# Window attention and spiking layer on one core: q and k projected a row further ahead, k's blocks placed by DMA, small tiles for maxima and picks

## The chip, the cores and the metric

The kernel runs on one core of a Trainium2 chip. The metric is the device time of one execution in microseconds, the median of several runs.

## The reference

`x` has 8 samples of 32 x 32 tokens with 256 channels.

```
x = x + attention(groupnorm(x))     # 8x8 windows, 16 heads of 16, bias table, mask -100
x = x + lif(groupnorm(x) @ W.T + b) # over the samples as time steps: charge, spike at >= 1, reset
attention: q, k, v = h @ qkv_w.T + qkv_b;  p = softmax(q*s @ k.T + bias + mask);  out = p @ v
```

A window has 64 tokens; four windows lie side by side in a window row, and the 8 samples have 32 such rows.

## The kernel before

Channels lie on the partitions (two halves `h` of 128), tokens in the free dimension. The attention goes through 32 window rows and, in each, two pairs of windows (`p` 0 and 1): 64 pairs, numbered `n`. The code of a sample is eight pairs long (`k` 0 to 7). Sample 0 and the last two are written out and the others are a loop. Every engine has its own `pair` function, a list in a fixed order, tied to the others by semaphores.

For a row, ACT normalises it (`normalise`, L478) and rounds it (`xn_high`, L490), POOL takes the rest (`low_part`, L403), and PE projects q, k (`project_q`, `project_k`, L918 to L923: 26 products of 128x256 4-byte elements) and v (`project_v`, L931 to L933: 12 products). q and k are then split into a high and a low f16 part: the high part by ACT (`q_high` L496, `k_high` L509), the low one by DVE (`q_low` L742, `k_low` L755). k is written twice, masked by the parity of the head (`parity_mask`), so that in each group of 32 channels one copy holds the even head and the other the odd one, with zeros between.

The score products (`scores`, L988 and L990, 32 per pair) need the three parts high x high, high x low, low x high under each other on 96 partitions. That is what `q_stack` and `k_stack` are (two slots of each). SP makes them through DRAM (`move_q_and_k`): it spills q and k (L321, L324, L315) and reads them back in stacks (L305). It also spreads q into `q_hi` (L311), whose zeros separate the heads for the maxima.

The softmax is made safe by a maximum for each query and head, taken one pair ahead: `max_scores` (L965 bias, L971 high parts) on PE, `maxima` (L772) on DVE, `turn_maxima` (L1005) on PE between the two halves of the next pair's scores, a copy into `max_rows` by ACT (L585), and at the end of the scores eight picks (L998), products that add the negated maximum of the right head to each score. ACT takes the exponential twice (L594 f32, L595 f16), POOL the rest (L441), PE multiplies with the values of the pair before (`weigh_values`, L1021), DVE divides (L786), PE turns the result (L1031), ACT keeps it (L558) and POOL adds it to x (L430).

In a pair PE does: the projection (q and k of the next row in even pairs, v of the next row in odd ones), scores with `turn_maxima`, picks, `weigh_values` of the pair before, `max_scores` of the next pair, `turn_attention`. After the attention the spiking layer runs through the 32 rows.

The two waits of `max_scores` and the one of `scores` are, in the code:

```
if k % 2 == 0:
    pe.wait_ge(k_hi_done, row + 1)
    pe.wait_ge(q_spread[slot], slot_total(row, k // 2, 64))
...
if p == 0:
    pe.wait_ge(stacked[slot], slot_total(row, k // 2, 96))
```

Of the kernel before, what the change touches and what calls it, by code (L numbers as in the profile page):

```python
# [3 lines left out]


def swin_attention_then_lif_kernel(nc, image, x, qkv_w, qkv_b, bias_table, lif_w, lif_b, out):
# [40 lines left out]
    with ctx:  # L47
# [3 lines left out]
        def sem(name):  # L51
# [14 lines left out]
        parity_mask = sb("parity_mask", [128, 2], f32)  # L66
        pick_max = sb("pick_max", [128, 2 * QUADS, 128], f16)
        bias_k = sb("bias_k", [128, 4, 2 * QUADS, 128], f16)
        bias_q = sb("bias_q", [128, 4, QUADS, 128], f16)
# [16 lines left out]
        bits = sb("bits", [128, 4], i32)  # L86
        flags = sb("flags", [128, 3], f32)
# [4 lines left out]
        q_hi = [sb(f"q_hi{i}", [128, HALVES, WCOLS, QUADS, WS], f16) for i in range(2)]  # L92
        q_stack = [sb(f"q_stack{i}", [96, QUADS, HALVES * WCOLS, WS], f16) for i in range(2)]
        k_stack = [sb(f"k_stack{i}", [96, QUADS, HALVES * WCOLS, 128], f16) for i in range(2)]
        q_spill = [[nc.dram_tensor(f"q_spill{i}{part}", [128, HALVES * ROWTOK], f16).ap() for part in ("hi", "lo")] for i in range(2)]
        k_spill = [[nc.dram_tensor(f"k_spill{i}{part}", [128, 2 * HALVES * ROWTOK], f16).ap() for part in ("hi", "lo")]
                   for i in range(2)]
        k_hi = [sb(f"k_hi{i}", [128, HALVES, WCOLS, 2, WS], f16) for i in range(2)]
        k_lo = [sb(f"k_lo{i}", [128, HALVES, WCOLS, 2, WS], f16) for i in range(2)]

        v_hi = [sb(f"v_hi{i}", [128, 2, HALVES * QUADS, 2, 2, D + 1], f16) for i in range(2)]
        v_lo = [sb(f"v_lo{i}", [128, 2, HALVES * QUADS, 2, 2, D + 1], f16) for i in range(2)]
# [52 lines left out]
        q_spread = [sem(f"q_spread{i}") for i in range(2)]  # L155
        q_hi_spilled = [sem(f"q_hi_spilled{i}") for i in range(2)]
        q_lo_spilled = [sem(f"q_lo_spilled{i}") for i in range(2)]
        k_hi_spilled = [sem(f"k_hi_spilled{i}") for i in range(2)]
        k_lo_spilled = [sem(f"k_lo_spilled{i}") for i in range(2)]
# [100 lines left out]
        BODY = 2 * WROWS  # L260

        W_SCALES = ((0, C, QK_SCALE), (C, 3 * C, 1.0))
# [22 lines left out]
        def _(sp):  # L285
# [58 lines left out]
            def pair(n, row, k, s):  # L344
# [4 lines left out]
                if k % 2 == 0 and not is_last_row(row):  # L349
                    move_q_and_k((k // 2 + 1) % 2, row + 1, k // 2 + 1)  # L350
# [112 lines left out]
        def _(act):  # L463
# [103 lines left out]
            def pair(n, row, k, s):  # L567
# [31 lines left out]
                if is_first(n, 2):  # L599
                    bias_high(2 + k)  # L600
# [528 lines left out]
```

## Time and profile before

| | us |
|---|---|
| median of 3 runs | 542.16 |
| lowest, highest | 538.04, 542.87 |
| the profiled execution's own time | 540.15 |
| its span, first to last instruction | 538.4 |
| PE, DVE, ACT, POOL busy in the span | 453.2, 426.7, 395.2, 274.1 |

The attention runs from the first pair at about 43 us to about 470 us, the spiking layer to the end. The span is 1.75 us shorter than the execution's time. Busy time is not work at full rate: products on PE are pipelined, each takes some 0.2 us from start to end and the next one starts 0.03 to 0.12 us after it.

### The profile page before, as it was taken

What the parts mean: (1) busy time and instruction counts of PE and PEld (TensorE: products, weight loads), DVE (VectorE), ACT (ScalarE), POOL (GpSimd) and SP (SyncE); (2) the same over time, 40 slices, a digit from 0 to 9 for tenths busy, and PEclk for the clock granted to TensorE, in tenths of its full rate; (3) what the DMA queues carried; (4) which work ended last, traced back from release to release, by engine and by line L of the source; (5) the groups of instructions that cost most, each with busy time, mean ns of one, the idle gap of its engine ahead of it and who ended that gap; (6) DMA issues with size and microseconds to landing.
All of it is one profiled execution on the core that took longest, in us unless ns stands there. A gap on an engine that the chain in (4) does not pass through costs nothing.

```text
span 538.4 us, 17562 instructions
## 1 busy us (share of the span) xinstructions
PE 453.2 (84%) x6504; PEld 415.6 (77%) x6504; DVE 426.7 (79%) x864; ACT 395.2 (73%) x885; POOL 274.1 (51%) x370
## 2 busy tenths in 40 slices
PE   0275689888989899989998999899899978789996
PEld 0164578887879788878888888899798867678885
DVE  6856568887887888878987898789877777588887
ACT  1375678887888788878887888788788856656551
POOL 6133565557555755666656656666665555540000
PEclk9988789999999999999999999999999989999999
DMA  6258066776777677767786788686666656023333
GB/s 191 83 142 199 12 177 167 185 191 168 186 180 176 172 179 197 188 170 182 202 203 156 198 196 195 159 196 162 160 157 168 163 144 157 2 84 133 136 136 138
DMA packets 92574, 86.07 MB, mean 160 GB/s; under 512 B 41842, under 2 KB 63604, under 8 KB 92532
## 3 DMA queue, kind: packets, MB, share of 16 engines
q1 hardware_dynamic: 91808, 85.49, 60.8%
q8 instruction: 27, 0.44, 0.4%
q10 hardware_dynamic: 724, 0.01, 0.1%
q14 instruction: 15, 0.12, 0.1%
HBM read 47.72 MB, written 33.55 MB: 151 GB/s over the span
## 4 chain that ended last, share of the span: by engine, by line
PE 36%; issue 17%; POOL 16%; ACT 10%; SPq 7%; DVE 7%; DMA 6%; ACTq 1%; POOLq 1%; DVEq 0%
POOL p_lo L441 7%; DMA k_stack<-k_spill1lo 4%; PE pv_ps L1021 4%; POOL xn_lo L403 3%; POOL xc L430 3%; PE score_ps L998 3%; PE proj_ps L921 3%; SPq L305 3%; SPq L311 3%; PE proj_ps L923 3%; PE proj_ps L908 3%; PE pv_ps L908 3%; PE score_ps L908 3%; PE proj_ps L922 3%; PE max_ps L908 2%
## 5 line engine op out<-in xcount | busy, mean ns | idle before, releaser
L441 POOL TENSOR_TENSOR p_lo<-probs,p_hi 128x512 f16<-128x512 f32 x128 | 146.6, 1167 | 151.9 <-ACT p_hi L595 151.9
L594 ACT ACTIVATE probs<-score_ps 128x512 f32<-128x512 f32 x128 | 76.9, 601 | 18.4 <-PE score_ps L998 17.6
L921 PE MATMUL proj_ps<-xn_hi,w_hi 128*128 128x256 f32 x256 | 77.0, 301 | 14.9 <-POOL xn_lo L403 14.9
L988 PE MATMUL score_ps<-both_parts,bias_k 128*128 128x64 f16 x1024 | 78.0, 193 | 11.7 <-DMA k_stack<-k_spill1lo 5.5
L988 PEld LDWEIGHTS score_ps<-both_parts,bias_k 128*128 128x128 f16 x1024 | 69.7, 98 | 16.8 <-issue 9.4
L772 DVE TENSOR_REDUCE neg_max<-max_ps 128x16 f16<-128x1024 f32 x64 | 78.4, 1225 | 3.7 <-PE max_ps L971 1.7
L990 PE MATMUL score_ps<-q_stack,k_stack 96*128 96x64 f16 x1024 | 77.7, 193 | 0.0
L595 ACT ACTIVATE p_hi<-score_ps 128x512 f16<-128x512 f32 x128 | 77.3, 604 | 0.0
L922 PE MATMUL proj_ps<-xn_lo,w_hi 128*128 128x256 f32 x256 | 74.1, 290 | 0.0
L923 PE MATMUL proj_ps<-xn_hi,w_lo 128*128 128x256 f32 x256 | 73.6, 287 | 0.0
L990 PEld LDWEIGHTS score_ps<-q_stack,k_stack 96*128 96x128 f16 x1024 | 69.1, 98 | 0.0
L755 DVE SCALAR_TENSOR_TENSOR k_lo<-proj_ps,parity_mask,k_hi 128x512 f16<-128x512 f32 x64 | 45.1, 746 | 26.8 <-ACT k_hi L509 26.8
L766 DVE TENSOR_TENSOR v_lo<-proj_ps,v_hi 64x256 f16<-64x256 f32 x128 | 54.1, 422 | 12.8 <-ACT v_hi L517 10.7
L921 PEld LDWEIGHTS proj_ps<-xn_hi,w_hi 128*128 128x128 f32 x256 | 50.3, 196 | 16.7 <-POOL xn_lo L403 9.8
L998 PE MATMUL score_ps<-max_rows,pick_max 128*128 128x128 f16 x512 | 40.5, 223 | 19.5 <-ACT max_rows L585 17.4
L517 ACT ACTIVATE v_hi<-proj_ps 64x256 f16<-64x256 f32 x128 | 50.5, 394 | 8.5 <-PE proj_ps L933 7.0
L786 DVE TENSOR_TENSOR attn<-pv_ps,recip 64x256 f32<-64x256 f32 x128 | 54.1, 422 | 3.1
L1021 PE MATMUL pv_ps<-v_hi,p_hi 128*128 128x68 f16 x512 | 55.6, 196 | 0.5 <-POOL p_lo L441 0.5
L1021 PE MATMUL pv_ps<-v_hi,p_lo 128*128 128x68 f16 x512 | 55.8, 196 | 0.0
L1021 PE MATMUL pv_ps<-v_lo,p_hi 128*128 128x68 f16 x512 | 55.7, 195 | 0.0
L509 ACT ACTIVATE k_hi<-proj_ps,parity_mask 128x512 f16<-128x512 f32 x64 | 40.5, 684 | 20.4 <-PE proj_ps L923 20.4
L403 POOL TENSOR_TENSOR xn_lo<-xn,xn_hi 128x512 fp32r<-128x512 f32 x32 | 41.1, 1285 | 22.8 <-ACT xn_hi L490 22.7
(137 smaller groups left out, 1354.6 us busy)
## 6 DMA issues: line engine op xcount, KB each, us to landing
xc<-in_x_dram SPq DMA_DIRECT2D x32, 256.0 KB, 4.9
k_stack<-k_spill0hi SPq DMA_DIRECT2D x32, 256.0 KB, 4.3
k_stack<-k_spill1hi SPq DMA_DIRECT2D x32, 256.0 KB, 4.3
out_dram<-xc SPq DMA_DIRECT2D x32, 256.0 KB, 2.3
q_hi<-q_flat SPq DMA_DIRECT2D x128, 32.0 KB, 2.0
k_spill0hi<-k_hi SPq DMA_DIRECT2D x16, 256.0 KB, 2.2
k_spill0lo<-k_lo SPq DMA_DIRECT2D x16, 256.0 KB, 2.3
q_stack<-q_spill0hi SPq DMA_DIRECT2D x32, 128.0 KB, 2.7
```

What stands on the lines that cost most here:

```text
L403: pool.tensor_tensor(xn_lo[slot][:, :], xn[slot][:, :], xn_hi[slot][:, :].bitcast(f32), ALU.subtract)\
L441: pool.tensor_tensor(p_lo[p][:, quads, :, :].rearrange("p g w i -> p (g w i)"), probs[:, quads, :, :].rearrange("p g w i -> p (g w i)"), p ...
L594: act.activation(probs[:, quads, :, :].rearrange("p g w i -> p (g w i)"), score_ps[:, h, :], ACT.Exp)
L595: act.activation(p_hi[p][:, quads, :, :].rearrange("p g w i -> p (g w i)"), score_ps[:, h, :], ACT.Exp)\
L772: dve.tensor_reduce(neg_max[:, 0:16], max_ps[:, :, :].rearrange("p w (n j) -> p (w n) j", j=WS), AX.X, ALU.max, negate=True).then_inc(neg_ ...
L908: last = pe.matmul(dst, w_lif[:, c, h * 128:(h + 1) * 128], tokens[:, c * ROWTOK:(c + 1) * ROWTOK], start=False, stop=(c == HALVES - 1))
L921: pe.matmul(dst, w_hi[:, c, cols], high[:, tok], start=(c == 0 and bias is None), stop=False)
L922: pe.matmul(dst, w_hi[:, c, cols], low[:, tok], start=False, stop=False)
L923: last = pe.matmul(dst, w_lo[:, c, cols], high[:, tok], start=False, stop=(c == HALVES - 1))
L988: pe.matmul(dst, bias_k[:, variant(k, w), h * QUADS + g, :], both_parts[:, 0, :], start=(g == 0 and w == 0), stop=False)
L990: pe.matmul(dst, k_stack[slot][:, g, at, :], q_stack[slot][:, g, at, :], start=False, stop=False)
L1021: last = pe.matmul(cols[:, :, g, :], pp[p][:, h * QUADS + g, :, :].rearrange("p w i -> p (w i)"), vv[k // 2][:, p, h * QUADS + g, :, :, :] ...
```

## The change

It has three parts.

- **Order.** q and k of row r + 2 are projected in the odd pair of row r, and v of row r + 1 in the even pair (before: q and k of row r + 1 in the even pair, v in the odd one). Normalising moves with it: `normalise` of row r + 3 at the end of ACT's odd pair, `xn_high` and `low_part` of row r + 2 in the even pair. v gets four buffers. On PE `max_scores` of the next pair stands right behind the picks, ahead of `weigh_values`, and its wait (now for the whole stack) stands before the last score product; on DVE `maxima` stands ahead of `attention_out`.
- **q and k.** k's high and low part are written once, flat, by one instruction each. The channels of q and k are permuted when the weights are prepared (4 x 3 small copies on ACT and on DVE in place of two large ones, four more small loads of biases), so that a stack is contiguous in DRAM for q. For k two DMAs per part put the even and the odd head's block into stacks that POOL has zeroed. A fourth group of 32 partitions is filled for half of the quads. q is no longer spread.
- **Tiles.** Maxima and picks use 64 rows and 64 columns of PE's array per product: 8 products of 256 columns for the bias and 16 of 128 for the scores' high parts (before: 2 of 512 and 8 of 128), and 16 picks of 128 (before: 8).

```
+            def stack_k(slot, first, part, quads=slice(0, QUADS)):
+                for e in range(2):
+                    rows = slice(first + e * D, first + (e + 1) * D)
+                    sp.dma_start(k_stack[slot][rows, quads, :, e * WS:(e + 1) * WS],
+                                 k_spill[slot][part][e * D:(e + 1) * D, quads, :].rearrange("d g (n j) -> d (g n) j", j=WS))\
+                      .then_inc(stacked[slot], 16)
+            def move_q_and_k(slot, r):
+                sp.wait_ge(q_flat_done, r + 1)
+                spill(q_flat, 0, q_hi_spilled, q_spill[slot][0])
+                sp.wait_ge(k_hi_done, r + 1)
+                spill(k_flat, 0, k_hi_spilled, k_spill[slot][0])
+                sp.wait_ge(k_lo_done, r + 1)
+                spill(q_flat, 1, q_lo_spilled, q_spill[slot][1])
+                if not is_first(r, 2):
+                    sp.wait_ge(score_ps_done, 4 * (r - 2) + 4)
+                spill(k_flat, 1, k_lo_spilled, k_spill[slot][1])
+                sp.wait_ge(q_hi_spilled, (r + 1) * 16)
+                stack_q(slot, 32, 0)
+                stack_q(slot, 64, 0)
+                stack_q(slot, 96, 0, slice(2, QUADS))
+                sp.wait_ge(k_hi_spilled, (r + 1) * 16)
+                stack_k(slot, 0, 0)
+                stack_k(slot, 32, 0)
+                stack_k(slot, 96, 0, slice(2, QUADS))
+                sp.wait_ge(q_lo_spilled, (r + 1) * 16)
+                stack_q(slot, 0, 1)
+                sp.wait_ge(k_lo_spilled, (r + 1) * 16)
+                stack_k(slot, 64, 1)
...
-                for e in range(2):
-                    last = act.activation(k_hi[slot][:, :, :, e, :].rearrange("p h w j -> p (h w) j"),
-                                          proj_ps[:, 1, :].rearrange("p (n j) -> p n j", j=WS), ACT.Identity,
-                                          scale=parity_mask[:, e:e + 1])
-                last.then_inc(k_hi_done, 1)
+                act.activation(k_flat[:, 0, :], proj_ps[:, 1, :], ACT.Copy).then_inc(k_hi_done, 1)
...
+            def max_scores(k):
+                slot = k // 2 % 2
+                halves = [slice(r * WS, (r + 1) * WS) for r in range(2)]
                 for w in range(2):
+                    for mid, rows in enumerate(halves):
+                        for q, queries in enumerate(halves):
+                            pe.matmul(max_ps[queries, mid, w * 256:(w + 1) * 256], ident_h[rows, rows],
+                                      bias_q[rows, variant(k, w), q, :, :].rearrange("p h n -> p (h n)"),
+                                      start=(w == 0), stop=False)
+                for w in range(2):
                     for h in range(HALVES):
+                        col = (2 * w + h) * 128
+                        at = h * WCOLS + 2 * (k % 2) + w
+                        for mid, rows in enumerate(halves):
+                            for q, queries in enumerate(halves):
+                                last = pe.matmul(max_ps[queries, mid, col:col + 128], q_stack[slot][rows, 2 * mid + q, at, :],
+                                                 k_stack[slot][rows, 2 * mid + q, at, :],
+                                                 start=False, stop=(w == 1 and h == 1))
...
+                for w in range(2):
+                    for h in range(HALVES):
+                        for mid, rows in enumerate(halves):
+                            for e, keys in enumerate(halves):
+                                dst = score_ps[keys, mid, :].rearrange("p (h q w i) -> p h w q i", h=2, q=2, w=2)[:, h, w, :, :]
+                                last = pe.matmul(dst, pick_max[rows, 2 * w + h, keys],
+                                                 max_rows[p][rows, :].rearrange("p (q i) -> p q i", q=2),
+                                                 start=False, stop=(w == 1 and h == 1))
+                            if w == 1 and h == 1:
+                                last.then_inc(score_ps_done, 1)
...
+                def await_tile_operands():
+                    pe.wait_ge(max_rows_done, n + 1)
+                    if not is_last_pair(n):
+                        await_max_operands(*following)
+                scores(n, row, k, await_tile_operands)
...
+                if not is_last_pair(n):
+                    max_scores(following[2])
                 if not is_first(n, 1):
+                    weigh_values(n - 1, row if p else row - 1, (k - 1) % BODY, beside)
```

PE before, in the loop, at the end of a pair: the last value products of the pair before, the maxima of the next pair (bias L965, scores L971), the turned attention, and the next projection.

```order
L1021 MATMUL pv_ps<-v_lo,p_hi 128x2x34
L1021 MATMUL pv_ps<-v_hi,p_lo 128x2x34
L960 REGISTER_ALU
L965 MATMUL max_ps<-bias_q,ident_h 128x512
L971 MATMUL max_ps<-k_hi,q_hi 128x128 x4
L965 MATMUL max_ps<-bias_q,ident_h 128x512
L971 MATMUL max_ps<-k_hi,q_hi 128x128 x4
L1031 MATMUL proj_ps<-ident,attn 128x128 x2
```

PE now, at the end of a pair's scores: the last score products (L1012, L1016), the picks (L1026), the maxima of the next pair (L987, L996) and the first value product.

```order
L1012 MATMUL score_ps<-both_parts,bias_k 128x64
L976 REGISTER_ALU
L1016 MATMUL score_ps<-q_stack,k_stack 128x64
L1026 MATMUL score_ps<-max_rows,pick_max 64x2x64 x16
L987 MATMUL max_ps<-bias_q,ident_h 64x256 x8
L996 MATMUL max_ps<-k_stack,q_stack 64x128 x16
L1040 REGISTER_ALU
L1050 MATMUL pv_ps<-v_hi,p_hi 128x2x34
```

The maxima moved ahead of the 24 value products and stand directly behind the picks; both read other operands and have more and smaller products.

SP before, one row in the loop: spills, spreads and stacks of one row.

```order
L321 DMA q_spill1hi<-q_flat 128x512
L311 DMA q_hi<-q_flat 32x8x64 x2
L324 DMA q_spill1lo<-q_flat 128x512
L315 DMA k_spill1hi<-k_hi 128x1024
L311 DMA q_hi<-q_flat 32x8x64 x2
L315 DMA k_spill1lo<-k_lo 128x1024
L305 DMA q_stack<-q_spill1hi 32x4x512 x2
L305 DMA k_stack<-k_spill1hi 32x4x1024 x2
L305 DMA q_stack<-q_spill1lo 32x4x512
L305 DMA k_stack<-k_spill1lo 32x4x1024
```

SP now, one row in the loop (L308 spills, L311 stacks of q, L317 stacks of k).

```order
L308 DMA q_spill1hi<-q_flat 128x512
L308 DMA k_spill1hi<-k_flat 128x512
L308 DMA q_spill1lo<-q_flat 128x512
L330 ISA
L308 DMA k_spill1lo<-k_flat 128x512
L332 REGISTER_ALU
L311 DMA q_stack<-q_spill1hi 32x2048 x2
L311 DMA q_stack<-q_spill1hi 32x1024
L317 DMA k_stack<-k_spill1hi 16x32x64 x4
L317 DMA k_stack<-k_spill1hi 16x16x64 x2
L311 DMA q_stack<-q_spill1lo 32x2048
L317 DMA k_stack<-k_spill1lo 16x32x64 x2
```

The four spreads are gone; k's three stacks of 2 KB pieces have become eight transfers of 128-byte pieces, of which six have 16x32 = 512 and two 16x16 = 256. The low part of k waits for the scores of the pair in which the row is projected.

## Rows read from the trace of the kernel before

**Rows 1.** One steady sample by stretches: us, busy us of engines, granted clock, DMA share, GB/s
```profile
286.67:337.66 50.99, 47.43 (x773) 43.81 (x773) 42.97 (x89) 43.16 (x101) 31.25 (x42) 1.00 0.75 186
```

**Rows 2.** Waits of PE from 108 to 467 us: us in total, times, longest
```profile
PE proj_ps L921 <- POOL xn_lo L403: 7.0, 6, 1.2
PE score_ps L998 <- ACT max_rows L585: 6.8, 17, 0.4
PE max_ps L1005 <- DVE neg_max L772: 5.8, 8, 1.0
PE score_ps L988 <- DMA k_stack<-k_spill1lo: 5.5, 6, 2.1
PE score_ps L988 <- DMA k_stack<-k_spill0lo: 4.0, 5, 1.8
PE pv_ps L891 <- DVE moments L686: 3.1, 1, 3.1
```

**Rows 3.** Timeline of PE within one pair: start, us
```profile
252.06 0.19 PE L990 MATMUL score_ps<-q_stack,k_stack 96*128 96x64 f16 x1
252.66 0.62 PE L998 MATMUL score_ps<-max_rows,pick_max 128*128 128x128 f16 x8 [0.42 <-ACT max_rows L585]
253.12 0.19 PE L1021 MATMUL pv_ps<-v_hi,p_hi 128*128 128x68 f16 x1
...
253.87 0.38 PE L965 MATMUL max_ps<-bias_q,ident_h 128*128 128x512 f16 x1
...
254.75 0.39 PE L1031 MATMUL proj_ps<-ident,attn 128*128 128x128 f32 x2
```

**Rows 4.** Timeline of ACT before the same picks
```profile
251.20 1.27 ACT L509 ACTIVATE k_hi<-proj_ps,parity_mask 128x512 f16<-128x512 f32 x2 [0.53 <-PE proj_ps L923]
252.36 0.25 ACT L585 ACTIVATE max_rows<-max_ps 16x128 f16<-16x128 f16 x1
```

**Rows 5.** Groups by line and shape: busy us, mean ns, idle before
```profile
L755 DVE SCALAR_TENSOR_TENSOR k_lo<-proj_ps,parity_mask,k_hi 128x512 f16<-128x512 f32 x64 | 45.1, 746 | 26.8 <-ACT k_hi L509 26.8
...
L509 ACT ACTIVATE k_hi<-proj_ps,parity_mask 128x512 f16<-128x512 f32 x64 | 40.5, 684 | 20.4 <-PE proj_ps L923 20.4
```

**Rows 6.** Timeline of SP's DMA issues within one row
```profile
189.54 0.43 SPq L315 DMA_DIRECT2D k_spill1hi<-k_hi  x1
190.01 1.26 SPq L311 DMA_DIRECT2D q_hi<-q_flat  x2
191.31 0.60 SPq L315 DMA_DIRECT2D k_spill1lo<-k_lo  x1
...
194.35 0.43 SPq L305 DMA_DIRECT2D k_stack<-k_spill1lo  x1
```

**Rows 7.** DMA issues: KB each, median us from issue to landing
```profile
k_stack<-k_spill0hi SPq DMA_DIRECT2D x32, 256.0 KB, 4.3
...
q_hi<-q_flat SPq DMA_DIRECT2D x128, 32.0 KB, 2.0
k_spill0hi<-k_hi SPq DMA_DIRECT2D x16, 256.0 KB, 2.2
```

**Rows 8.** The start: chain, PE's first maxima, SP's first stack, PE's wait for max_rows
```profile
4.40 8.23 DMA probs<-in_qkv_b_dram
...
36.21 0.38 PE L965 MATMUL max_ps<-bias_q,ident_h 128*128 128x512 f16 x1 [3.68 <-ACT bias_q L525]
...
34.83 0.94 SPq L305 DMA_DIRECT2D q_stack<-q_spill0hi  x2
...
PE score_ps L998 <- ACT max_rows L585: 10.6, 3, 5.2
```

**Rows 9.** Timeline of PE in a projection with 4-byte weights
```profile
248.86 0.28 PE L923 MATMUL proj_ps<-xn_hi,w_lo 128*128 128x256 f32 x1
248.98 0.28 PE L921 MATMUL proj_ps<-xn_hi,w_hi 128*128 128x256 f32 x1
```

More of the change, by code:

```diff
@@ L3 @@
 from contextlib import ExitStack
+import itertools
 def swin_attention_then_lif_kernel(nc, image, x, qkv_w, qkv_b, bias_table, lif_w, lif_b, out):
@@ L433, in pair @@
                 p = k % 2
-                if p == 1 and not is_last_row(row, 2):
+                if p == 0 and not is_last_row(row, 2):
                     low_part(k // 2 % 2, row + 3)
@@ L533, in _ @@
             for first, end, scale in W_SCALES:
-                act.activation(w_hi[:, :, first:end], w_raw[:, :, first:end], ACT.Copy, scale=scale).then_inc(setup_act, 1)
+                for c, h in itertools.product(range(HALVES), range(HALVES)):
+                    last = act.activation(w_columns(w_hi, first, c, h, True), w_columns(w_raw, first, c, h, False), ACT.Copy, scale=scale)
+                last.then_inc(setup_act, 1)
             act.activation(w_lif[:, :, :], w_raw[:, :, 3 * C:OUTS], ACT.Copy, scale=1.0 / TAU)
@@ L598, in pair @@
                     keep_attention(n - 2, p)
+                if is_first(n, 1):
+                    v_high(1, 2, 0)
+                    v_high(1, 2, 1)
+                if p == 1 and not is_last_row(row, 3):
+                    sample = s + (k // 2 + 3) // WROWS
+                    normalise(row + 3, sample, nxt % 2, sample + 1, row + 3)
                 if is_first(n, 2):
@@ new lines, in scores @@
+                for mid in range(2):
+                    wait(pe, p_hi_done, n * 2 + (mid - 1))
+                    for h in range(HALVES):
+                        for q in range(2):
+                            for w in range(2):
+                                col = (2 * h + q) * 128 + w * WS
+                                dst = score_ps[:, mid, col:col + WS]
+                                at = h * WCOLS + 2 * p + w
+                                pe.matmul(dst, bias_k[:, variant(k, w), h * QUADS + 2 * mid + q, :], both_parts[:, 0, :],
+                                          start=(h == 0 and q == 0 and w == 0), stop=False)
+                                if (mid, h, q, w) == (1, 1, 1, 1):
+                                    before_tiles()
+                                pe.matmul(dst, k_stack[slot][0:96, 2 * mid + q, at, :], q_stack[slot][0:96, 2 * mid + q, at, :],
+                                          start=False, stop=False)
+                    if mid == 0:
+                        turn_maxima(n)
```

339 lines of the change are left out of this document (146 added, 193 removed).

## The prediction

> **What bounds the kernel now.** First the view of the span by stretches, for one sample of the steady part [rows 1]. The reader is to see three things in it: the sample takes 50.99 us, PE is busy for 47.43 of them at a granted clock of 1.00 (the upper level, 2.4 GHz), while DVE and ACT have 8 us to spare and POOL 20. So PE's stream of instructions sets the pace, and the time is what PE issues plus what it waits for. The waits follow [rows 2], from the first steady sample (108 us) to the last pair (467 us): 7.0 us for POOL's xn_lo, 6.8 for ACT's max_rows, 5.8 for DVE's neg_max, 5.5 and 4.0 for the last transfer into k_stack, 3.1 for the moments of the last norm. That is 32.2 us of 359, over 28 rows; the rest is issue. The timeline of one pair [rows 3] shows what is issued: from the picks on, 0.46 us for eight picks, 0.75 us for 24 value products, 0.88 us for the score products of the next pair's maxima. It also shows a stretch without work of 0.6 us (252.06 to 252.66) between the last score product and the first pick.
>
> **The change on PE.** Per pair it takes away 8 picks and 10 products for maxima, which are 0.46 + 0.88 = 1.34 us [rows 3], and puts 16 picks and 24 products on 64x64 tiles in their place, 40 in all. No product on a part of the array that another product could share in time is in this trace, so the price is bounded. From the columns: 2048 columns for maxima took 0.88 us, 0.43 ns each [rows 3]. The new ones stream 16 x 128 + 8 x 256 + 16 x 128 = 6144 columns. If the four tiles work at once this is 1536 columns, 0.66 us per pair, or -0.68 x 64 pairs = -43 us; if nothing overlaps it is 2.64 us, +1.30 x 64 = +83 us. The nearest row is the smallest product with its own weights: 24 value products from 253.12 to 253.87, 31 ns each although they stream only 68 columns [rows 3]. I take this as what a load of weights and a short product cost together: 40 x 31 = 1.25 us, -0.09 x 64 = -6 us.
>
> **The change in the waits.**
> - *xn_lo*: normalising and splitting a row now comes a half row before the q projection that reads it (its low part on POOL in the even pair, the projection in the odd one). The 7.0 us go. Next late is the norm of the next sample, which must be ready at the end of pair 3 instead of at pair 4.
> - *neg_max*: the maxima of pair n + 1 are now multiplied right after the picks of pair n and reduced before the attention output. They come about 0.75 us earlier on PE and 1.2 us earlier on DVE, more than the usual lateness: 5.8 us go.
> - *max_rows*: k's high part was two ACT instructions, 1.27 us on ACT's queue ahead of max_rows [rows 4, 5], and becomes one. Its group says 684 ns each, so some 0.6 us of the queue go, and max_rows starts when it is turned. A part stays in every pair, since the turned maxima must go through ACT and back; in [rows 3] the wait was 0.42, and I leave a third of it: -5 of the 6.8 us.
> - *k_stack*: the stacks are filled one row further ahead, so the 9.5 us go if SP keeps up. This is the dearest condition. SP issued 15 transfers a row, and now issues 17: 4 spills, 4 of q, 8 of k, one of x. Such an issue takes 0.43 us where it moves 128 pieces, and 0.63 us each where it moves 256 pieces of 128 bytes (the spread of q, two in 1.26 us) [rows 6]. Six of the new k transfers move 512 pieces of 128 bytes, two move 256. An issue of 512 lies between 0.43 us (the count does not matter) and 0.43 + 3 x 0.20 = 1.03 us (each further 128 pieces cost what the first ones did). I take 0.63, the nearest row. From the start of the projection of q and k the k_low spill may start after about 5.3 us (3.2 us of projection, 1.0 us of scores, 0.3 to 0.6 us of waiting, 0.46 us of picks, for it now waits for the scores of this pair to free the slot). Then SP needs 0.45 for it, 4 x 0.47 for q, 8 x 0.63 for k: 12.7 us. A transfer of 128-byte pieces landed after 2.0 us, the k stacks after 4.3 [rows 7], so all is there at 14.7 to 17.0 us. PE asks after one row and 4.3 us more; with a row of 11.9 us that is 16.2. It just holds. What is queued behind that wait on PE is everything: the last score product, picks, maxima.
>
> A rule of the Trainium skill speaks against these pieces: its page "DMA: Bandwidth & Descriptors", Specifications, wants at least 512 B per piece for full rate. The spread's 32 KB landed in 2.0 us against 2.2 for 256 KB of k in 2 KB pieces [rows 7], so small pieces do lose rate here. That the load on the 16 engines stays bearable follows from the share of 0.75 [rows 1] and the fewer bytes.
>
> Together -7.0 - 5.8 - 5 - 9.5 = -27 us.
>
> **What it adds.** DVE loses one of its two k_low passes (746 ns, [rows 5]), which only shortens the chain to SP. When PE stops waiting, ACT is next: in the sample it was busy 43.16 us, and loses 4 x 0.6; a sample of 47.4 - 0.4 + small waits leaves it 6 us free, but the even pair, with v's four copies, is the tight one. I give back 3 us for it. At the start the first maxima were multiplied at 36.21 us, right after q's spread [rows 8]; now they wait for all 12 stack transfers. SP began its stacks at 34.83 us [rows 8]; 4 x 0.47 + 8 x 0.63 = 6.9 us and a landing put the first maxima at about 44 us, 8 us later, and the projection of the second row stands behind them. Part of this is taken up, since PE waited 10.6 us for max_rows there while the bias tables were made, which goes on beside it. The start itself waited till 12.63 us for the small loads of the biases (begun at 4.40, [rows 8]), behind four more issues now. I take +5 us for the start, from 0 to +10. The 12 small copies of the permuted weights lie beside the first statistics.
>
> **Sum**, against the profiled execution's 540.15 us (2.0 us below the median of the runs shown): 540.15 - 6 - 27 + 3 + 5 = 515 us. Against the median it would be 517; I say 516.
>
> **Rivals.**
> 1. *The tiles work four abreast* (chance 0.22). For it: the fixed cost of a product is not tied to its columns in [rows 3], so the columns could vanish. Against it: 31 ns looks like a floor. Then 43 us go instead of 6: 515 - 37 = 478, but the even pair then runs into ACT, of which I keep 10 us: 488.
> 2. *SP comes too late* (0.20), the case on the slow side. One mechanism: the eight k issues. At 1.03 us for 512 pieces the chain above is 5.3 + 0.45 + 1.9 + 6 x 1.03 + 2 x 0.63 = 15.1 us, and 17.1 to 19.4 with landing, against 16.2 that PE leaves. With 3 us of landing each row is 1.9 us too long, 28 x 1.9 = +53 over 515, or 568; halfway to the bound it is about 548. The rows are hidden up to an issue of 0.72 us, and from 0.87 us on (0.9 us per row, 25 us in all) nothing of the gain is left. For it: an issue of 256 pieces did take longer than one of 128 [rows 6]. Against it: the issue after a spread takes 0.60 too, so it may be a matter of form, not of count.
> 3. *Weights of a tile load at the slow rate* (0.10). Products with 4-byte weights of 128 columns follow at 0.12 us [rows 9] though their 256 columns need only 0.11 at 0.43 ns. If tile weights load like these and one after another, half the columns take 60 ns: 40 x 60 = 2.4 us per pair, +1.06 x 64 = +68 where I took -6: 589.
> 4. *The waits only change their names* (0.10): the arrays' change of shape and ACT take back what goes, 0.2 us per pair and the rest in waits for max_rows: 540.
>
> Rival 3 is also what the Trainium skill would have: "TensorEngine Tiling (Array Packing)", Restrictions and Gotchas, says that column tiling excludes the fast load of weights, and "TensorE: Matmul & The Clock Gate", LDWEIGHTS, prices a load by its columns, which for 64 columns would be an estimated 53 ns. The trace agrees in that 2-byte weights of 128 columns keep a 31 ns rhythm and 4-byte ones do not. The first page also says that tiles load and multiply in parallel, which is rival 1.
>
> **How the numbers follow.** The forecast (505 to 530) has 0.38, rivals 1 to 4 0.22, 0.20, 0.10 and 0.10. The predicted time is the forecast's, 516. About 1% is what a measurement of this kernel can tell from no change. Faster by more: the forecast, rival 1 and 0.02 of the milder end of rival 2: 0.62. Within 1%: most of rival 4 and a part of rival 2, 0.13. Slower: the rest, 0.25. The range takes in rival 1 and the milder half of rival 2, and leaves rival 3 out: 485 to 562.
>
> **What would show it.** In the profile of the changed kernel: PE's waits for xn_lo and neg_max gone from the list; 16 picks and 24 maxima products from first to last in about 1.25 us per pair (0.7 is rival 1, 2.4 is rival 3); a steady sample of about 47.5 us; no wait for a k_stack transfer; SP's issues of k near 0.63 us. The first maxima near 44 us. The forecast is wrong if SP has no idle time within a row, or if PE's wait before the last score product of odd pairs names a k_stack transfer in the steady samples.

## The result, and the profile after

| | before | after |
|---|---|---|
| median of the runs, us | 540.88 (538.04 to 542.87) | 547.35 (546.37 to 548.88) |
| profiled execution, us | 540.15 | 546.64 (span 544.9) |

The ratio is 1.0117 (95% interval 1.0069 to 1.0165): the changed kernel is slightly slower. 516 us were predicted, with 0.62 on faster. Times here and below are medians of all executions of a kernel, while a ratio and its interval leave out those that are over 1.5% above the fastest of their kernel; so the 540.3 us of the first experiment stand beside a ratio of 0.9948.

The waits of PE from 113 to 472 us, the answer to [rows 2]:

```profile
PE score_ps L1016 <- ACT max_rows L598: 28.9, 23, 1.5
PE proj_ps L949 <- issue: 11.4, 4, 3.0
PE score_ps L1016 <- DMA k_stack<-k_spill1lo: 5.3, 6, 3.0
PE score_ps L1016 <- DMA k_stack<-k_spill0lo: 4.9, 6, 1.5
PE pv_ps L909 <- DVE moments L703: 0.8, 1, 0.8
PE max_ps L1034 <- DVE neg_max L785: 0.2, 1, 0.2
```

xn_lo and neg_max have gone from the list, as forecast. The wait for max_rows has grown from 6.8 to 28.9 us, the k_stack waits are 10.2 where they were 9.5, and there is a new kind: four waits of nearly 3 us before the v projection with no releaser at all ("issue": the profile shows nothing that PE waited for). The sum is 51 us, where it was 32.

The timeline of PE in one pair, the answer to [rows 3]:

```profile
379.48 0.20 PE L1016 MATMUL score_ps<-q_stack,k_stack 96*128 96x64 f16 x1 [1.31 <-ACT max_rows L598]
379.62 0.42 PE L1026 MATMUL score_ps<-max_rows,pick_max 64*64 64x128 f16 x16
379.86 0.39 PE L987 MATMUL max_ps<-bias_q,ident_h 64*64 64x256 f16 x8
380.08 0.39 PE L996 MATMUL max_ps<-k_stack,q_stack 64*64 64x128 f16 x16
380.41 0.20 PE L1050 MATMUL pv_ps<-v_hi,p_hi 128*128 128x68 f16 x1
```

Read the starts, not the durations: 16 picks, 8 bias products and 16 score products take from 379.62 to 380.41, 0.79 us, where the old ones took 1.34. So the tiles are cheap. By the single starts four products begin together; the next four follow 0.056 us later where a product has 128 columns, and 0.11 us later where it has 256, so columns set the pace and not the loads of weights. But ahead of them PE stands 1.31 us for max_rows. ACT over the same stretch, the answer to [rows 4]:

```profile
376.66 1.12 ACT L493 ACTIVATE xn<-xc,shift,rstd 128x256 f32 x2
377.82 0.63 ACT L506 ACTIVATE xn_hi<-xn 128x512 fp32r<-128x512 f32 x1
378.35 0.77 ACT L529 ACTIVATE v_hi<-proj_ps 64x256 f16<-64x256 f32 x2
379.15 0.28 ACT L598 ACTIVATE max_rows<-max_ps 128x128 f16<-128x128 f16 x1
```

The maxima were turned at 377.5; the normalising, xn_hi and the first half of v_hi stand ahead of their copy in ACT's queue. This is the even pair; in the odd one ACT is idle for nearly 2 us. k's copies are cheaper, as forecast: one of 0.60 us on ACT and one pass of DVE, the answer to [rows 5]:

```profile
L773 DVE TENSOR_TENSOR k_flat<-proj_ps,k_flat 128x512 f16<-128x512 f32 x32 | 22.1, 690 | 7.0 <-ACT k_flat L524 7.0
```

SP's issues of one row (the last column counts the issues that the duration spans), and the landing of the k stacks, the answers to [rows 6, 7]:

```profile
239.90 0.35 SPq L308 DMA_DIRECT2D q_spill1hi<-q_flat  x1
240.31 0.42 SPq L308 DMA_DIRECT2D k_spill1hi<-k_flat  x1
240.78 0.46 SPq L308 DMA_DIRECT2D q_spill1lo<-q_flat  x1
242.37 0.32 SPq L308 DMA_DIRECT2D k_spill1lo<-k_flat  x1
242.81 2.70 SPq L311 DMA_DIRECT2D q_stack<-q_spill1hi  x3
245.56 3.72 SPq L317 DMA_DIRECT2D k_stack<-k_spill1hi  x6
249.31 0.45 SPq L311 DMA_DIRECT2D q_stack<-q_spill1lo  x1
249.81 2.43 SPq L317 DMA_DIRECT2D k_stack<-k_spill1lo  x2
...
k_stack<-k_spill1lo SPq DMA_DIRECT2D x32, 64.0 KB, 3.3
```

In this row 12.3 us pass from the first spill to the end of the last issue (10.3 to 13.0 in the others); there is a gap of 1.1 us before the k_low spill, where SP waits for the slot. The spans of three and of two issues, 2.70 and 2.43 us, hide something. Single issues into k_stack from 110 to 465 us, shortest, median and longest in ns, before and after:

```profile
L305 SPq DMA_DIRECT2D k_stack<-k_spill1hi x28: 430/432/438, 113.4 to 452.6; - x28
L317 SPq DMA_DIRECT2D k_stack<-k_spill1hi x84: 447/626/1805, 113.1 to 454.5; - x84
L317 SPq DMA_DIRECT2D k_stack<-k_spill1lo x28: 544/627/1897, 117.4 to 457.4; - x28
```

Most issues of 512 pieces take 0.63 us, as the prediction had it. But 47 of SP's 449 issues in this stretch take 1.0 to 2.1 us, where it was 10 of 391 before; in the row above it is one of the q issues and one of the k_low ones, 1.84 us each. Why these are long is open. How much room is left on SP is told by its wait for the next row's q, before and after:

```profile
SPq L321 <- ACT q_flat L496: 115.7, 26, 8.9
SPq L308 <- ACT q_flat L512: 14.6, 12, 3.0
```

Before, SP was done ahead of the next q in 26 of 28 rows and waited 4.4 us each time in the mean. Now rows take 12.4 to 13.5 us, and it is done ahead of the next q in 12 of 28.

Samples by stretches, the answer to [rows 1]: a looped one, and the last but one, which is written out in the program:

```profile
275.00:327.70 52.70, 45.65 (x952) 43.00 (x950) 39.24 (x84) 40.90 (x97) 31.37 (x41) 0.95 0.54 131
377.50:426.90 49.40, 43.69 (x954) 41.21 (x951) 37.62 (x80) 40.72 (x97) 31.14 (x42) 1.00 0.51 119
```

PE's busy time at the full clock has fallen from 47.43 to 43.69 us a sample. The written-out sample is 1.6 us shorter than one of before, the four looped ones at whose end the loop turns (52.7 to 54.1) are 2 to 3 longer. The fifth looped one, which has no turn behind it, takes 49.8. What happens at the first turn, at 162 us, in steps of 2 us (clock: third number from the end), and the wait itself:

```profile
162.00:164.00 2.00, 0.22 (x2) 0.00 (x0) 1.92 (x6) 2.00 (x6) 2.00 (x2) 1.00 0.56 148
164.00:166.00 2.00, 0.97 (x8) 0.98 (x9) 0.98 (x4) 0.89 (x2) 1.72 (x3) 1.00 0.38 82
166.00:168.00 2.00, 2.00 (x31) 1.90 (x31) 0.35 (x1) 0.97 (x3) 0.37 (x1) 0.60 0.41 61
168.00:170.00 2.00, 2.00 (x54) 1.73 (x52) 1.49 (x5) 1.65 (x5) 0.00 (x0) 0.55 0.57 107
170.00:172.00 2.00, 2.00 (x35) 2.00 (x36) 1.83 (x5) 1.83 (x5) 1.61 (x2) 1.00 0.53 98
```

```profile
165.03 0.38 PE L949 MATMUL proj_ps<-w_hi,xn_hi 128*128 128x256 f32 x1 [2.81 <-issue]
```

PE stands still for 2.81 us, works on, and then the granted clock is at its lower level (1.2 GHz) for most of four microseconds. The same follows each of the four turns: the missing shares of the clock over the 2 us steps add up to 8.5 us of lost time, in the loop of before to nothing. A hint at the wait is the queue that brings instructions to the engines. From 165 to 300 us it carries no packet in the trace of before, and in that of after:

```profile
q8 instruction: 23, 0.38, 1.3%
```

At the start the forecast held: the first maxima were multiplied at 45.18 us (44 forecast), after the wait below, the answer to [rows 8], and the second sample began 4.7 us later than before (5 forecast).

```profile
PE max_ps L987 <- DMA k_stack<-k_spill0lo: 10.4, 1, 10.4
```

### The profile page after: what moved, and what is told of

Read it like the earlier page. It is cut to its first block, busy times and chain, and to the rows that moved or that the text cites. A ratio compares the mean times of both kernels' runs of the same rounds, so it can differ in the third digit from the quotient of the medians.

```text
span 544.9 us, 20474 instructions
## 1 busy us (share of the span) xinstructions
PE 434.2 (80%) x7912; PEld 403.4 (74%) x7912; DVE 398.2 (73%) x838; ACT 377.4 (69%) x863; POOL 280.3 (51%) x382
## 4 chain that ended last, share of the span: by engine, by line
PE 38%; SPq 21%; ACT 11%; DMA 10%; issue 9%; DVE 8%; ACTq 1%; POOL 0%; DVEq 0%; POOLq 0%
SPq L317 12%; SPq L311 7%; DMA k_stack<-k_spill0lo 4%; PE pv_ps L1050 4%; PE proj_ps L939 3%; DMA k_stack<-k_spill1lo 3%; PE proj_ps L940 3%; PE proj_ps L941 3%; PE score_ps L1026 3%; PE score_ps L1016 3%; PE proj_ps L926 3%; PE pv_ps L926 3%; PE score_ps L926 3%; ACT xn L493 2%; ACT v_hi L529 2%
## 5 line engine op out<-in xcount | busy, mean ns | idle before, releaser
L1016 PE MATMUL score_ps<-q_stack,k_stack 96*128 96x64 f16 x1024 | 88.1, 197 | 50.5 <-ACT max_rows L598 39.2
L1016 PEld LDWEIGHTS score_ps<-q_stack,k_stack 96*128 96x128 f16 x1024 | 74.2, 100 | 56.8 <-ACT max_rows L598 47.7
L779 DVE TENSOR_TENSOR v_lo<-proj_ps,v_hi 64x256 f16<-64x256 f32 x128 | 54.2, 423 | 59.3 <-ACT v_hi L529 58.4
L1012 PE MATMUL score_ps<-both_parts,bias_k 128*128 128x64 f16 x1024 | 80.8, 197 | 0.0
L1012 PEld LDWEIGHTS score_ps<-both_parts,bias_k 128*128 128x128 f16 x1024 | 72.8, 100 | 2.8
L1050 PEld LDWEIGHTS pv_ps<-v_hi,p_hi 128*128 128x128 f16 x512 | 49.4, 101 | 5.5 <-POOL p_lo L454 1.0
L940 PEld LDWEIGHTS proj_ps<-xn_lo,w_hi 128*128 128x128 f32 x256 | 50.8, 198 | 0.0
L941 PEld LDWEIGHTS proj_ps<-xn_hi,w_lo 128*128 128x128 f32 x256 | 50.5, 197 | 0.0
```

The costliest lines, as they stand in the source:

```text
L940: pe.matmul(dst, w_hi[:, c, cols], low[:, tok], start=False, stop=False)
L941: last = pe.matmul(dst, w_lo[:, c, cols], high[:, tok], start=False, stop=(c == HALVES - 1))
L1012: pe.matmul(dst, bias_k[:, variant(k, w), h * QUADS + 2 * mid + q, :], both_parts[:, 0, :], start=(h == 0 and q == 0 and w == 0), stop=False)
L1016: pe.matmul(dst, k_stack[slot][0:96, 2 * mid + q, at, :], q_stack[slot][0:96, 2 * mid + q, at, :], start=False, stop=False)
L1050: last = pe.matmul(cols[:, :, g, :], pp[p][:, g // 2 * 4 + h * 2 + g % 2, :, :].rearrange("p w i -> p (w i)"), vv[k // 2][:, p, h * QUADS ...
```

## The experiments

Three theories stood at first: A, the loop's body no longer stays with PE and is fetched at each turn; D, ACT's queue in the even pair makes PE late; E, the chain of SP's issues does. B, C and F are named in the expectations. Kernel 7 is the kernel of experiment 7, and so on. Each kernel is compared with runs of the kernel before on the same chip.

**1. The loop written out** (after, one edit).

```diff
-            with eng.Fori(1, SAMPLES - 2) as s:
-                for k in range(BODY):
-                    body(s * BODY + k, s * WROWS + k // 2, k, s)
-            for s in (SAMPLES - 2, SAMPLES - 1):
+            for s in range(1, SAMPLES):
```

> The changed kernel with its loop over samples 1 to 5 written out in the program, nothing else. Theory A (the loop's body, 952 products a sample instead of 773, no longer stays with TensorE and is fetched again at each turn: four waits before the v projection with no releaser, 11.4 us in all): these waits go, 547.4 becomes about 536; if the slower pace of the looped samples (53.5 us each against 49.6 of the written-out ones) is the fetch too, 527. Rival B (the waits at the turn only take the place of others, and the pace is set by ScalarE and the stacks): 545 to 549, with other waits at the same places. Rival C (straight code is fetched all the time as well, at its own price): 547 or more, with waits without a releaser spread over the samples.

540.3 us (533.0 to 542.6, 10 runs), 0.9948 [0.9907, 0.9989] of before. The waits without a releaser are gone; those for max_rows and the k stacks have grown from 38 to 52 us (both from 112 to 470 us):

```profile
PE score_ps L1013 <- ACT max_rows L595: 33.9, 27, 1.4
PE score_ps L1013 <- DMA k_stack<-k_spill0lo: 9.1, 8, 2.0
PE score_ps L1013 <- DMA k_stack<-k_spill1lo: 8.7, 8, 1.9
```

So A is right that these waits come with the loop, and B about more than half of their worth in this kernel: of 11.4 + 8.5 us, 7 to 9 came out as time.

**2. The kernel before with about as many products as after** (control for A: 969 a sample, after 952): each maxima product cut in two, each pick in four or two.

```diff
+                            for e in range(2):
+                                last = pe.matmul(max_ps[:, w, at + e * WS:at + (e + 1) * WS],
...
+                            parts = 4 - 2 * w
+                            for c in range(parts):
```

> The kernel before with the products of its maxima cut in two and those of its picks in four or two, 24 more products a pair and the same columns, so that its loop body is as long as that of the changed kernel (which has 22 more a pair). Theory A: the instruction queue, quiet in the loop of before, carries packets all through the loop and TensorE waits without a releaser at the four turns; 540.9 becomes 550 or more (11 for the fetch, up to 5 for the cut products). Rival: the length of the body means nothing, no such waits, and 541 to 546 by the cuts alone.

582.2 us, 1.0747 [1.0678, 1.0815]. The instruction queue is at work in the loop, and the first line of PE's waits is

```profile
PE proj_ps L921 <- issue: 19.8, 4, 5.1
```

Before had no such line. The four looped samples with a turn take 59.3 to 61.0 us, the two behind the last turn 52.6 and 53.0 (before 50.7 and 51.6), so the turns cost some 30 us: 19.8 of waits, and the rest goes with the lower clock, whose missing shares add up to 12. The cut products cost 1.6 a sample. Here only the number of products was changed, and the waits came: that they hang on the size of the loop's body is shown, at a price above the expectation. That the wait is a fetch is read from the queue's packets.

**3. Full-array picks in the changed kernel** (looped; 8 products of 128x128 in place of 16 tiles).

```diff
-                            for e, keys in enumerate(halves):
-                                last = pe.matmul(dst, pick_max[rows, 2 * w + h, keys],
+                            last = pe.matmul(dst, pick_max[:, 4 * mid + 2 * w + h, :],
```

> The changed kernel, in its loop, with eight picks over the full 128x128 array a pair instead of sixteen in 64x64 tiles; the maxima's 24 products stay tiles. Price of a tile: eight full picks stood at 0.46 us a pair in the kernel before, sixteen tile picks take 0.247 us, so TensorE's busy time rises by 0.21 x 64 = 14 us (by nothing if tiles only overlap in pairs, as the prediction had it: 16 x 31 ns = 0.50). The loop's body has 64 products a sample fewer (888 against 952 and 773 before): if its length decides the fetch in proportion, the waits without a releaser at the turns fall from 11.4 to about 7 us; if there is a size from which all of it is fetched again, they stay at 11 or vanish. Time: 547 to 560.

554.2 us, 1.0214 [1.0122, 1.0306]. The eight picks last from 391.65 to 392.20, 0.55 us against 0.247 for 16 tiles (379.62 to 379.86 above): the tiles overlap four abreast.

```profile
391.65 0.61 PE L1024 MATMUL score_ps<-max_rows,pick_max 128*128 128x128 f16 x8
392.20 0.41 PE L986 MATMUL max_ps<-bias_q,ident_h 64*64 64x256 f16 x8
```

The waits without a releaser did not shrink with the body (15.9 us in all at 888 products a sample, 11.4 at 952, none at 779). That reads as a size from which the body is fetched, between 779 and 888 products, each with its load of weights; these are two different kernels, and nothing between was run.

**4. The kernel before, written out** (control; the edit of 1).

> The kernel before, written out, as a control: its loop showed no packet of the instruction queue and no wait without a releaser. Theory A: 540.9 stays within 3 us, since there is nothing to gain and straight code runs without a stall. If straight code costs by itself, it is slower by over 3 us.

548.4 us, 1.0107 [1.0042, 1.0172]: a miss, straight code is not free here. No wait lacks a releaser; the k_stack waits rose from 9.5 to 17.0 us. Why the stacks land later is open.

**5. ACT's normalising earlier** (after, looped): its two operations move ahead of k's copy in the odd pair.

```diff
                     q_high(row + 3)
+                    if not is_last_row(row, 3):
+                        normalise(row + 3, sample, nxt % 2, sample + 1, row + 3)
                     k_high(row + 3)
```

> The changed kernel with ScalarE's two normalising operations (1.12 us) moved from the end of the odd pair into its idle time ahead of k's copy. Theory D (in the even pair ScalarE's queue, normalise + xn_hi + v_hi ahead of max_rows, makes TensorE's last score product late by 28.9 us in all): that wait falls by about 1 us a row, 20 to 28 us in all, and the time falls by 12 to 25 us, to 522 to 535. Rival E (the row's period is set by the stacks, which SyncE issues too late: 9 of its issues of 512 pieces at 0.62 to 0.83 us): the max_rows wait falls, the k_spill waits before the maxima's products grow by as much, and the time stays within 3 us of 547.

573.5 us, 1.0614 [1.0559, 1.0669], against both theories. The edit made a wait of its own: in the second row of a sample the normalising needs the next sample's scales, which POOL has not done:

```profile
191.02 1.09 ACT L493 ACTIVATE xn<-xc,shift,rstd 128x256 f32 x2 [4.15 <-POOL shift L237]
```

Behind it stand k's copy and max_rows, so PE stands still from 188.61 to 192.88, and its clock is at half from 190 to 197, so it falls before PE goes on. This comes in each sample: six ACT waits of 23.9 us, and the granted clock is 0.88 to 0.92 in four samples. PE's busy time rose from 434 to 447 us for the same products.

**6. The same, written out** (the edits of 1 and 5).

> Both edits, loop written out and normalise early. If theories A and D hold and are independent their gains add: 547 - 11 - 12 to 25 = 511 to 524. If one hides behind the other (both stand on the same chain of a row), the time is that of the better one of the two, 525 to 536. If E holds for the row's period, about that of the written-out kernel alone.

562.7 us, 1.0363 [1.0303, 1.0423]. Writing out takes some 11 us off kernel 5; the wait for the scales is there too. It tells nothing on D and E.

**7. Normalising early in three rows of four** (written out).

```diff
-                    if not is_last_row(row, 3):
+                    if k != 3 and not is_last_row(row, 3):
```

> The changed kernel written out, with the two normalising operations ahead of k's copy in three rows of four; in the second row of each sample they stay behind, since there they would wait for the next sample's scales (the ScalarE wait of 4.2 us that the first try of this had in each sample). Theory D (ScalarE's queue in the even pair): the max_rows wait falls from 33.9 to some 10 us and the time from 540.3 to 515 to 525. Rival E (SyncE's issues and the landing of the stacks set the row): the k_stack waits grow from 17.8 us by as much as the max_rows wait falls; 535 to 542. Theory F (the clock, granted at half for some 4 us behind each stall of TensorE of nearly 3 us): no window of 2 us below 0.98 in the steady part, since no wait of over 2 us is left.

538.2 us (534.6 to 544.7), 0.9912 [0.9870, 0.9954]. The max_rows wait fell by 22 us and the k_stack waits rose by 14:

```profile
PE score_ps L1016 <- DMA k_stack<-k_spill0lo: 18.3, 13, 2.5
PE score_ps L1016 <- DMA k_stack<-k_spill1lo: 13.4, 9, 3.5
PE score_ps L1016 <- ACT max_rows L598: 11.8, 18, 1.4
```

So D's wait is real, but its end is worth 2 us, which the intervals of kernels 1 and 7 can't tell from nothing, and the k_stack waits take its place, as E has it. SP is the fuller for it: it is done ahead of the next q in 4 rows.

```profile
SPq L305 <- ACT q_flat L509: 2.5, 4, 1.2
```

F failed: the clock fell three times in the steady samples, at 214, 330 and 368 us, behind k_stack waits of 2.25, 1.55 and 1.77 us.

**8. SP's chain relieved**: kernel 7, where the stacks' rows 96 to 127 are not loaded any more from the third row on, one q and two k transfers a row less. The products still read them, so for half of the heads the maxima leave out this row's high product.

```diff
-                stack_k(slot, 96, 0, slice(2, QUADS))
+                if r < 2:
+                    stack_k(slot, 96, 0, slice(2, QUADS))
...
```

(the q transfer likewise)

> The same, and from the third row on the stacks' rows 96 to 127 are not loaded any more (one q and two k transfers a row less, of 9 SyncE issues of 512 pieces... two less); what is left out is the high product of half the heads in the maxima. It prices SyncE's chain: three issues less are 0.46 + 2 x 0.79 = 2.0 us a row on SyncE. Rival E: the k_stack waits go, and the time is 10 to 25 us under that of the kernel that loads them. Theory D alone: the same within 3 us.

504.5 us (501.8 to 508.8), 0.9333 [0.9251, 0.9414], 34 us under kernel 7. The k_stack waits are down from 31.7 to 4.6 us, and all steady samples look alike:

```profile
295.10:341.10 46.00, 43.63 (x953) 41.16 (x950) 39.40 (x86) 40.30 (x97) 31.26 (x42) 1.00 0.61 141
```

E is shown for a kernel whose ACT order is mended: PE is busy for as long as in kernel 7, but is not kept waiting. SP is done ahead of the next q in 18 rows (20.4 us of waiting). Two things stay open. The three transfers have gone from the DMA engines too, and not only their issues from SP; kernel 11 bears on that. And the same relief with ACT's order as in the changed kernel was not run, so how much of the 34 us needs both is not known.

**9. The kernel before, relieved alike**: two of its six stack transfers a row left out from the third row on, and with them two parts of the scores' operands. That is 0.9 us of SP a row, where kernel 8 has some 2.0.

```diff
-                stack(1, k_stack[slot], k_spill[slot][0])
+                if is_first(row, 2):
+                    stack(1, k_stack[slot], k_spill[slot][0])
```

(likewise `stack(2, q_stack[slot], q_spill[slot][0])`)

> The kernel before with two of its six stack transfers a row left out from the third row on (third q part and second k part of the scores' sum: left out of the computation), 0.43 us of SyncE each. The same relief of the chain that gave the changed kernel 34 us. If TensorE bounds the kernel before (47.2 us of 51 a sample), only the k_stack waits of 8.4 us can go: 530 to 541. If the stacks' chain set the pace there too, 505 to 525, and the change's gain on TensorE was not hidden by a bound that it brought itself.

536.9 us (535.3 to 538.5), 0.9918 [0.9890, 0.9947]. Its k_stack waits shrank to 0.2 us (its max_rows waits grew from 6.8 to 11.2), and nothing more was to be had:

```profile
208.90:259.90 51.00, 47.33 (x778) 43.88 (x775) 42.98 (x89) 43.11 (x101) 31.21 (x41) 1.00 0.60 154
```

This is the clearest comparison of the study. With the chain out of the way, the kernel before takes 51.0 us a sample and the changed one (with ACT's order mended, written out) 46.0, 536.9 against 504.5 us. The gain is there, and the chain that came with the change hides it: before, PE was the bound, and SP had time to spare.

**10. Kernel 8 in its loop** (the edit of 1 taken back).

> The kernel without the stacks' rows 96 to 127 (what is left out is the high product of half the heads in the maxima), in its loop instead of written out, the only difference from the kernel of 504.5 us. There TensorE is the bound (46 us a sample, 43.6 busy), so the fetch at the turns has its full price: four waits of 2.8 to 3 us and half the clock for some 4 us behind each, 11.4 + 8.5 = 20 us: 520 to 528. Rival: the waits are made good by slack (as most of them were in the changed kernel, where writing out gave 7 us): 508 to 512.

523.9 us, 0.9668 [0.9615, 0.9721]: 19.4 us over kernel 8 for the loop alone, more than twice as much as in experiment 1, since here little else is waited for. PE's waits without a releaser are 14.5 us, and a looped sample shows the clock:

```profile
161.70:212.30 50.60, 44.80 (x951) 42.16 (x949) 39.25 (x84) 40.18 (x97) 31.22 (x41) 0.97 0.56 127
```

**11 to 14. A version that keeps the whole computation.** Kernel 7 with the four q transfers of a row issued by POOL (11), the same issued behind xn_lo (12), that with max_rows ahead of the first v_hi on ACT (13), and that with POOL's issues back behind p_lo and the addition of the attention behind xn_lo (14).

```diff
...
+                    pool.wait_ge(q_hi_spilled, (row + 3) * 16)
+                    stack_q(pool, q_stacked[slot], slot, 32, 0)
+                    stack_q(pool, q_stacked[slot], slot, 64, 0)
+                    stack_q(pool, q_stacked[slot], slot, 96, 0, slice(2, QUADS))
+                    pool.wait_ge(q_lo_spilled, (row + 3) * 16)
+                    stack_q(pool, q_stacked[slot], slot, 0, 1)
```

For 13, on ACT:

```diff
-                if v_now:
-                    v_high(nxt, row + 2, 0)
                 act.wait_ge(max_turned, n + 1)
                 act.activation(max_rows[p][:, :], max_ps[:, 0, :].bitcast(f16)[:, 0:128], ACT.Copy)\
                     .then_inc(max_rows_done, 1)
                 if v_now:
+                    v_high(nxt, row + 2, 0)
                     v_high(nxt, row + 2, 1)
```

For 14, on POOL:

```diff
                     low_part(k // 2 % 2, row + 3)
+                if p == 0 and not is_first(n, 3):
+                    add_attention(n - 3, row - 2, 1)
```

> The same as the early normalising in three rows of four, with the four q transfers of a row issued by GpSimd instead of SyncE (1.8 us a row off SyncE's chain, nothing left out). Rival E: the k_stack waits fall by 1 to 2 us a row against the kernel that issues all from SyncE, 5 to 20 us in all. Against it: GpSimd issues slower than 1 us a transfer, p_lo comes late, and pv_ps waits for it: the time is 5 to 20 us worse.

> The written-out kernel with the early normalising and the four q transfers from GpSimd, now issued behind xn_lo in the next pair instead of ahead of it (2.0 us of GpSimd's issues stood before xn_lo, and TensorE waited for xn_lo 25.0 us in all, once a row). If that wait only came from the order on GpSimd, it falls to under 5 us and the time from 530.9 to 507 to 517, as the k_stack waits stay away. If the later q transfers become the last to land, a wait for q_stack or k_stack takes its place and the time stays at 525 to 532. Nothing is left out.

> The kernel with the later q transfers, and on ScalarE max_rows ahead of the first v_hi in the even pair (0.77 us). If ScalarE's queue is what is left of the max_rows wait (12 us), it falls to under 6 us and the time by 3 to 8 us; if v_lo and through it the next q projection become late by it (v_lo on VectorE, then the wait of TensorE on v_lo), the same within 2 us.

> The kernel of 529.3 us (written out, early normalising, max_rows first) with GpSimd's q transfers issued at once behind p_lo of the odd pair (there no stack was waited for), and the addition of the attention put behind xn_lo (0.74 us earlier xn_lo). If the row is now set only by the order on GpSimd, q_stack and k_stack waits fall from 19.6 to under 5 us, the xn_lo wait is 5 to 18 us (1.3 less 0.74 us a row), and the time is 510 to 525. If the stacks' chain sets it whatever GpSimd does, 526 to 532 with the waits under other names.

| kernel | us | ratio to before | what PE waits for most, us |
|---|---|---|---|
| 11 | 530.9 | 0.9811 [0.9744, 0.9878] | xn_lo 25.0, max_rows 12.6, k_stack 1.9 |
| 12 | 532.0 | 0.9796 [0.9741, 0.9852] | q_stack 21.5, max_rows 12.0, k_stack 7.1 |
| 13 | 529.3 | 0.9781 [0.9719, 0.9843] | k_stack 14.8, v_lo 10.8, q_stack 4.8 |
| 14 | 526.0 | 0.9725 [0.9677, 0.9773] | xn_lo 20.0, no releaser 7.2, k_stack 4.8 |

Kernel 11 takes nothing out, only moves 1.8 us a row off SP, and the k_stack waits fall from 31.7 to 1.9 us. A row on SP takes some 9 us there, where it was 11 to 13 in kernel 7, and SP waits 69.8 us in all for q: the stacks were late by SP's time, and not by what the transfers put on the DMA engines. (In part they have more time, too: PE stands 1.0 us a row for xn_lo, ahead of the projection that they follow.) POOL's 2.0 us stand ahead of xn_lo now; issued later, as in 12, they make the q transfers the last to land. Kernel 13 missed the 3 to 8 us (the intervals overlap with 12), though the max_rows wait fell to 3.9 us. Kernel 14 is the best that computes everything: it beats the kernel before by 2.7% and the changed one by about 21 us. Its steady samples take 49.4 us in the mean, where kernel 8, which loads less, takes 46.0.

## Why the prediction was wrong, by its own steps

- *Tiles, -6 us.* Failed, in its size: the value products' 31 ns a product were taken for a floor. 40 products took 0.79 us a pair, not 1.25, and 16 tile picks 0.247 against 0.55 for 8 full ones. Rival 1, four abreast at 0.66, was the nearer. By the starts this is 0.55 x 64 = 35 us, by PE's busy time per sample (47.43 to 43.69) 30.
- *xn_lo and neg_max, -7.0 and -5.8.* Right.
- *max_rows, -5.* Failed: +22. The step looked at k's copy, which is in the odd pair. In the even pair the normalising, xn_hi and half of v's copies came to stand ahead of max_rows; the 3 us that the sum gave back for ACT are the same step, and far too few. Kernel 7 showed that 22 us of the wait can be taken away by order alone, and that by itself this is worth 2 us or nothing.
- *k_stack, -9.5.* Failed, +0.7, and this is the step that decides: with the loop written out and ACT's order mended, taking three issues a row away is worth 34 us. The sum of 14.7 to 17.0 us against 16.2 was called holding. It took 6.9 us for the 12 issues of the stacks, each at its usual price. That price was near (0.63 us for most of the long k issues; rival 2's slow end was 1.03), but one issue in ten takes 1.0 to 2.1 us, so the 12 take 8.1 in the mean. In the row shown the q projection begins at 235.9 us and the last issue ends at 252.2, 16.4 us later, where the sum had 12.7. A row of 11.9 us was assumed, and those of the changed kernel take 12.4 and more. Rival 2 named this chain as the danger, but by a price per issue that did not come, and priced it from 515; in truth the tiles' gain was there for it to eat. Kernels 8, 9 and 11 show it.
- *Code fetch, not in the sum.* 11.4 us of waits and 8.5 of half clock. The count of PE's instructions a sample was in the prediction's own terms (22 more a pair), and nobody asked where the loop's code lives. Kernels 1, 2 and 10 show it.
- *Start +5.* Right: 4.7.
- *Rival 3* (slow weights, 589) is out.
- *Small pieces lose rate.* 32 KB in 2.0 us against 256 KB in 2.2 does not tell this from a time that every transfer takes. In the changed kernel 64 KB of k in 128-byte pieces land 3.2 to 3.5 us after their issue, 64 KB of q 2.8: the pieces cost at most some 0.6 us a transfer.

With the measured sizes the sum is 540.15 - 30 (tiles) - 7.0 - 5.6 - 2.3 (moments, 3.1 to 0.8) + 22.1 + 0.7 + 11.4 + 8.5 + 4.7 = 542.7, against 546.6. Of the missing 4 us, 1.3 are in the end of the kernel behind the last pair, and 1.7 go with the last sample's lower clock (0.92 where it was 0.96); the rest was not traced. The sum takes waits as if they added; kernels 1 and 7 show that they only do so in part.

The Trainium skill's page "TensorEngine Tiling (Array Packing)", Restrictions and Gotchas, excludes the fast load of weights for column tiles, and rival 3 took a slow pace from it. Whatever the load's form, the trace shows no cost of it here: four products with their own weights of 64 columns start together, and the next four about 56 ns later, which is what 128 columns take at 0.43 ns. What the same page says on tiles that load and multiply in parallel is what these rows show.

## What to carry to other kernels

Before a change takes time off the bounding engine, add up the chain that feeds it, issue by issue, and against the shorter row that the change itself makes; a chain that just holds will be the next bound. An instruction count is a cost too: ask for the size of a loop's body, and read the instruction queue in the loop. And a stall of PE of nearly 3 us mostly cost more than itself here, as the lower clock came with it. Last, look at single issues beside their usual price: with the long ones the stacks' issues took 8.1 us a row, where the usual price gave 6.9.

## What the runs showed of the hardware that was not expected

- A loop body of 779 products a sample on PE ran without instruction packets, one of 888 or more brought some 1 every 6 us and a wait of 2.8 to 5.1 us at each turn. Straight code is fetched too (62 packets in kernel 1), with no such wait.
- 40 products on 64x64 tiles, each with its own weights, took 0.79 us: 20 ns a product.
- With nearly every stall of PE of 2.8 us and more the granted clock went to half for 3.4 to 7 us, beginning in the stall or up to 5 us behind it, whoever caused the stall (ACT, a transfer, the fetch). It did not behind one of 2.86 us in kernel 3 and one of 2.86 us in kernel 5. In kernel 1 it fell twice behind waits of 1.6 and 2.0 us. In kernels 11, 13 and 14, whose steady waits are mostly at or under 1.5 us, it did not fall in the steady samples.
- An issue of 512 pieces of 128 bytes took SP 0.63 us in the median; 47 of 449 issues of all kinds took 1.0 to 2.1 us, where the kernel before had 10 of 391. The cause is open. POOL issued q transfers at 0.50 us each.
